# Routed sums in a PSUM bank of their own, and the blocks of additions, the value copy and the output addition at other places

## What is computed

```
# attention: 16 heads, window of 64 tokens, 16 numbers per head and token ("bond")
disp  = xn @ W_disp ; val = xn @ W_val
strain[t, d] = disp[t - 63 + d] - disp[t]                     # d = 0..63
bond    = gelu(strain @ W_strain + rel_pos_emb[d] @ W_pos) @ W_bond
damage  = sigmoid(gelu(strain @ W_dmg + b_dmg) @ W_dmg_out + b_dmg_out)
weights = softmax over d of (bond - 10 * damage)              # masked where t - 63 + d < 0
out     = (sum over d of weights * val[t - 63 + d]) @ W_cproj

# experts: 160, the 8 best of each token
gate  = top-8 of sigmoid(xn @ router_w.T + expert_bias), normed, * 2.5
h     = silu(xn @ w_gate[e])
routed[t] = sum over its 8 experts of gate * (h @ w_down[e])  # plus one shared expert
```

## Time and profile before

| | |
|---|---|
| median of 3 runs | 3710.76 us (3703.95 to 3714.79) |
| the profiled execution's own time | 3708.35 us |
| its span, first to last instruction | 3706.8 us |
| mean granted TensorE clock | 0.844 of full speed |
| busy share of the span: TensorE, VectorE, ScalarE, GpSimd | 67%, 77%, 67%, 63% |

### The profile page before, as it was taken

One profiled execution on the slowest core, in us unless ns is written; L12 is line 12 of the kernel. 1 busy time (PEld: TensorE's weight loads), 2 busy tenths in 40 slices (PEclk: granted clock), 3 DMA queues, 4 the chain that ended last, 5 costly groups with the idle time before them and its releaser, 6 DMA issues. The chain is left out here.

```text
span 3706.8 us, 64220 instructions
## 1 busy us (share of the span) xinstructions
PE 2501.0 (67%) x21226; PEld 1211.9 (33%) x21226; DVE 2861.7 (77%) x4254; ACT 2500.9 (67%) x1716; POOL 2327.2 (63%) x1604
## 2 busy tenths in 40 slices
PE   4662666776676766767888885566666676667666
PEld 2441112222222222246666661122222222222224
DVE  6888988888888888822433337999999899989981
ACT  1111979988888888843333337878878877778883
POOL 1222888678787878823343437777777777667771
PEclk9886879888888898868999997878778877878885
DMA  6773122222222222226878872222222222222222
GB/s 247 284 277 129 38 78 84 90 88 85 68 86 86 84 97 76 77 89 195 243 243 244 242 241 74 70 78 73 81 70 84 71 82 76 75 82 78 77 69 88
DMA packets 366243, 435.33 MB, mean 117 GB/s; under 512 B 48673, under 2 KB 282993, under 8 KB 366066
## 3 DMA queue, kind: packets, MB, share of 16 engines
q1 hardware_dynamic: 284658, 278.53, 24.0%
q0 software_dynamic: 57216, 143.22, 11.6%
q10 hardware_dynamic: 24192, 11.02, 1.1%
HBM read 233.83 MB, written 198.77 MB: 117 GB/s over the span
## 5 line engine op out<-in xcount | busy, mean ns | idle before, releaser
L1069 DVE SCALAR_TENSOR_TENSOR u_dve<-s_win,rpos,ps_here 128x512 f32<-128x512 f32 x1792 | 1197.6, 740 | 213.4 <-PE ps_l L1153 107.6
L1153 PE MATMUL ps_l<-u_dve,wsel 128*32 128x512 f32 x6144 | 984.8, 770 | 392.6 <-ACT u_dve L993 186.1
L927 POOL TENSOR_TENSOR u_pool<-s_win 128x4096 f32<-128x4096 f32 x128 | 1021.7, 7982 | 7.5 <-DMA s_win<-s_dram 5.3
L993 ACT ACTIVATE u_dve<-u_dve 128x4096 f32<-128x4096 f32 x224 | 809.9, 3616 | 56.8 <-DVE u_dve L1069 56.7
L1064 DVE TENSOR_TENSOR u_dve<-s_win,ps_here 128x4096 f32<-128x4096 f32 x160 | 703.3, 4412 | 43.1 <-PE ps_l L1153 43.1
L915 POOL DMA_INDIRECT yg<-yslot_dram,slot_now x512 | 485.6, 948 | 285.7 <-issue 148.5
L906 POOL DMA_INDIRECT xslot_dram<-xr,slot_now x512 | 494.6, 966 | 147.0 <-issue 143.6
L991 ACT ACTIVATE u_pool<-u_pool,bdmg_sb 128x4096 f32<-128x4096 f32 x128 | 474.5, 3707 | 66.1 <-POOL u_pool L927 66.1
L991 ACT ACTIVATE u_dve<-u_dve,bdmg_sb 128x4096 f32<-128x4096 f32 x128 | 474.4, 3706 | 15.8 <-DVE u_dve L1064 15.5
L1153 PEld LDWEIGHTS ps_l<-u_dve,wsel 128*32 128x32 f32 x6144 | 194.8, 128 | 842.8 <-issue 549.8
L1014 ACT ACTIVATE at_sb<-ps_u 128x512 f32<-128x512 f32 x256 | 151.0, 590 | 375.3 <-PE ps_u L1216 301.7
(11 more groups left out here) (142 smaller groups left out, 3011.1 us busy)
## 6 DMA issues: line engine op xcount, KB each, us to landing
band<-band_dram SPq DMA_DIRECT2D x32, 2048.0 KB
xslot_dram<-zero SPq DMA_DIRECT2D x16, 2688.0 KB, 9.1
xs<-xslot_dram SPq DMA_DIRECT2D x168, 256.0 KB, 3.6
yslot_dram<-ys POOLq DMA_DIRECT2D x168, 256.0 KB, 3.2
band_dram<-ml SPq DMA_DIRECT2D x64, 512.0 KB
we<-in_w_expert SPq DMA_DIRECT2D x336, 64.0 KB, 2.8
s_win<-s_dram SPq DMA_DIRECT2D x64, 288.0 KB, 5.9
s_dram<-s_sb POOLq DMA_DIRECT2D x16, 1024.0 KB, 4.7
```

Source lines behind the costliest of these rows:

```text
L927: pool.tensor_tensor(item_buffer(n), windows(par, ty, d0, 8), s_win[:, par, ty, PAD:PAD + TC].unsqueeze(1).to_broadcast([P, 8, TC]), ALU.s ...
L993: act.activation(u, u, ACT.Gelu).then_inc(gelu_done, 1)
L1069: last = dve.scalar_tensor_tensor(out=item_buffer(n)[:, d, :], in0=s_win[:, par, ty, d0 + d + 1:d0 + d + 1 + TC], scalar=rpos[:, d0 + d:d0 ...
L1153: last = pe.matmul(ps_l[32 * g:32 * g + 32, cgrp % 2, ty, :], wsel[:, ty, q, :], item_buffer(n)[:, d, :], start=(q == 0), stop=(q == 3))
```

## The change

Three things, all in `attend`. First, the damage logits get a single bank `ps_d` instead of two of `ps_l`, and the bank that is left over is `ps_acc`. TensorE's first damage product of a group waits for the tanh of the group before, and ScalarE does that tanh ahead of gelu n (n % 4 = 1) instead of behind it. Second, `add_routed` starts its sums with a multiplication into `ps_acc`, adds there, and ends each pair with one addition of `ps_acc` to `acc`, ahead of which (no longer at the start) it waits for the base; a pair counts 17 on `sum_round` instead of 16. Pair 1 moves from n = 11 to n = 7, and pair 0 from n = 3 to n = 15 of the step before. Third, on GpSimd the value copy moves from n = 3 to n = 7, and the output addition from n = 5 to n = 12.

```diff
-            ps_l = c.enter_context(nc.psum_tensor(f"ps_l_{half}", [P, 2, 2, TC], F32))
+            ps_l = c.enter_context(nc.psum_tensor(f"ps_l_{half}", [P, 2, TC], F32))
+            ps_d = c.enter_context(nc.psum_tensor(f"ps_d_{half}", [P, TC], F32))
+            ps_acc = c.enter_context(nc.psum_tensor(f"ps_acc_{half}", [P, J, C], F32))
...
+            ROUND = 2 * TOPK + 1
...
 # store_routed (SyncE); route on GpSimd, bring and gates on ScalarE count in the same way
-                        if some(NS * (t - 1)):
-                            sp.wait_ge(sum_round, NS * (t - 1))
+                        if some(2 * ROUND * (t - 1)):
+                            sp.wait_ge(sum_round, 2 * ROUND * (t - 1))
...
 # GpSimd
-                            if "a" in st and n == 3 and par == 0:
+                            if "a" in st and n == 7 and par == 0:
                                 spread(it - 1)
-                            if "y" in st and n == 5:
+                            if "y" in st and n == 12:
...
 # ScalarE: the same block, behind the gelu of item n before, ahead of it now
+                            if n % 4 == 1 and ("i" in st if n > 1 else "s" in st):
+                                k = 4 * s + cgrp - 1
+                                act.wait_ge(item_done, 4 * k + 4)
+                                if some(k - 1):
+                                    act.wait_ge(logits_in, k - 1)
+                                act.activation(tanh_sb[:, (cgrp - 1) % 2], ps_d[:], ACT.Tanh,
+                                               bias=hbout[:], scale=0.5).then_inc(tanh_done, 1)
...
 # VectorE, add_routed
                         if pair == 0:
-                            if some(16 * t):
-                                dve.wait_ge(base_in, 16 * t)
-                            if some(t):
-                                dve.wait_ge(gates_here, t)
+                            dve.wait_ge(gates_here, t)
                         for j in (2 * pair, 2 * pair + 1):
-                            if some(16 * TOPK * t):
-                                dve.wait_ge(gathered[j], 16 * TOPK * t)
+                            dve.wait_ge(gathered[j], 16 * TOPK * t)
+                        before = 2 * ROUND * (t - 1) + ROUND * pair
                         for m in range(2 * TOPK):
                             j = 2 * pair + m % 2
                             i = j * TOPK + m // 2
-                            if m >= 2:
-                                dve.wait_ge(sum_round, NS * (t - 1) + 2 * TOPK * pair + m - 1)
-                            dve.scalar_tensor_tensor(
-                                out=acc[:, old, j, :], in0=yg[:, i, :], scalar=gate_now[:, old, i:i + 1],
-                                in1=acc[:, old, j, :], op0=ALU.mult, op1=ALU.add).then_inc(sum_round, 1)
+                            if m < 2:
+                                dve.tensor_scalar(ps_acc[:, j, :], yg[:, i, :], gate_now[:, old, i:i + 1], None,
+                                                  ALU.mult).then_inc(sum_round, 1)
+                            else:
+                                dve.wait_ge(sum_round, before + m - 1)
+                                dve.scalar_tensor_tensor(
+                                    out=ps_acc[:, j, :], in0=yg[:, i, :], scalar=gate_now[:, old, i:i + 1],
+                                    in1=ps_acc[:, j, :], op0=ALU.mult, op1=ALU.add).then_inc(sum_round, 1)
+                        if pair == 0:
+                            dve.wait_ge(base_in, 16 * t)
+                        dve.wait_ge(sum_round, before + ROUND - 1)
+                        dve.tensor_tensor(acc[:, old, 2 * pair:2 * pair + 2, :], ps_acc[:, 2 * pair:2 * pair + 2, :],
+                                          acc[:, old, 2 * pair:2 * pair + 2, :], ALU.add).then_inc(sum_round, 1)
...
 # VectorE, step
-                            if half == 1 and "s" in st and n % 8 == 3:
-                                add_routed(s - first, 1 - par, n // 8)
+                            if half == 1 and "s" in st and n == 7:
+                                add_routed(s - first, 1 - par, 1)
+                            if half == 1 and "i" in st and n == 15:
+                                add_routed(s - first + 1, par, 0)
...
 # TensorE
-                                if n % 4 < 2:
+                                if n % 4 == 0:
                                     if some(4 * s + cgrp - 1):
                                         pe.wait_ge(logits_in, 4 * s + cgrp - 1)
+                                if n % 4 == 1:
+                                    if some(4 * s + cgrp):
+                                        pe.wait_ge(tanh_done, 4 * s + cgrp)
                                 pe.wait_ge(gelu_done, NI * s + n + 1)
...
-                                    last = pe.matmul(ps_l[32 * g:32 * g + 32, cgrp % 2, ty, :], wsel[:, ty, q, :],
+                                    logit = ps_d if ty else ps_l[:, cgrp % 2]
+                                    last = pe.matmul(logit[32 * g:32 * g + 32, :], wsel[:, ty, q, :],
                                                      item_buffer(n)[:, d, :], start=(q == 0), stop=(q == 3))
```

More of the change, by code:

```diff
@@ L911, in route @@
                             if some(s - first):
-                                pool.wait_ge(sum_round, NS * (s - first - 1) + 2 * TOPK * (j // 2 + 1))
+                                pool.wait_ge(sum_round, 2 * ROUND * (s - first - 1) + ROUND * (j // 2 + 1))
                                 pool.sem_inc(held, 1)
@@ L956, in bring @@
                         else:
-                            if some(NS * (s - first - 1)):
-                                act.wait_ge(sum_round, NS * (s - first - 1))
+                            if some(2 * ROUND * (s - first - 1)):
+                                act.wait_ge(sum_round, 2 * ROUND * (s - first - 1))
                                 act.sem_inc(held, 1)
@@ L993, in step @@
                                     act.activation(u, u, ACT.Gelu).then_inc(gelu_done, 1)
[L995 to L1001, removed]
                             if n == 13 and "i" in st and (not isinstance(s, int) or s + 1 < end):
@@ L1083, in step @@
                                                          in0=tanh_sb[:, (cgrp - 2) % 2], scalar=-5.0,
-                                                         in1=ps_l[:, (cgrp - 2) % 2, 0], op0=ALU.mult,
+                                                         in1=ps_l[:, (cgrp - 2) % 2], op0=ALU.mult,
                                                          op1=ALU.add).then_inc(logits_in, 1)
```

## The result

| | before | after |
|---|---|---|
| median of the runs, us | 3710.9 | 3666.2 |
| ratio after / before, 95% interval | | 0.9883 [0.9854, 0.9913] |
| profiled execution, own time / span | 3708.35 / 3706.8 | 3657.13 / 3655.7 |
| first half, 13 steps | 1025.2 | 1037.7 |
| second half, first Exp to last but one, 14 steps | 1229.2 | 1169.2 |

The change saves 45 us in the medians, 51 in the profiled executions; the prediction was 46. But it does not come as forecast: the second half gains 60 us, and the first half, which was to stay as it is, loses 12.5. The rest of the program (from one half to the other, start and end) is 3.6 us shorter.

The account below looks back on a forecast made before the run. It took the second half as bound by VectorE's gapless stretch including pair 1 (10.02 us), then ScalarE's gelu chain. Terms 104 - 72 + 14 = 46 us saved gave 3665 us on the median's scale; range 3628 to 3704.

Parts of the forecast that it names:

- Pairs at 4.8 us: VectorE's additions in the second half: with sums in PSUM, no hold-up, 4.8 us a pair (4.8 to 7.2).
- rival (a): VectorE's additions: writing PSUM is slow, up to 36 us less gain, 3701; chance 0.14.
- Pair 1 leaves n = 11, +104: Spot after the third `ml`, second half: removing pair 1 saves its time less 2.8 a step, 104 us.
- Pair 1 at n = 7, -72: Between subtractions 6 and 8, VectorE's gapless stretch: pair 1 costs 15 x 4.8 = 72 us, to 108.
- Pair 0 at n = 15, +14: Leaving n = 3 wins 2.0 us in seven odd steps; the wait for `ps_here` covers the new place: 14 us.
- Tanh before gelu, 0: ScalarE: delay at n = 9 covered by the band-transpose wait; at most 0.6 a step elsewhere, 19 us; taken as 0.
- Rival (c): Tanh order lands on the path, 3.2 us in 32 steps, 102 us slower, 3767; chance 0.06.
- GpSimd's moves and the windows, 0: GpSimd loses three waits and runs ahead; windows land just in time, then some 9 us earlier: 0.
- Rival (b): Windows come late for TensorE, `ps_here` waits 4.5 us in odd steps, 63 us more, 3728; chance 0.10.
- Rival (e): GpSimd's lateness was on the path, up to 66 us more gain, half of it gives 3632; chance 0.12.
- Rival (d): Additions still held: pair 1 at n = 7 costs 9.7 + 0.5, 81 us more, 3746; chance 0.03.
- Of what was to show it: Second-half signs: 4.8 us pairs, none over 0.5, band wait about 5, no `ps_here` wait, steps 85; first half 78.9.

Follow-up runs that it names:

- 1: Changed kernel with both pairs back at n = 3 and 11, sums still in PSUM: ratio 0.9867 to before, median 3658.5 us.
- 2: Kernel before with only the pairs moved to the new places, sums in SBUF: ratio 1.0121 to before, median 3756.2 us.
- 8: As 5, but pair 1 back at n = 11, pair 0 staying at n = 15: ratio 0.9748 to before, median 3615.1 us.
- 10: As 8, but tanh ahead of the gelu in the first half: ratio 0.9823 to before, median 3640.4 us.
- 5: Changed kernel with the first half as before (two damage banks, tanh behind gelu, GpSimd's steps back): ratio 0.9831 to before, median 3646.2 us.
- 6: Changed kernel with two damage banks in the first half again: ratio 0.9879 to before, median 3665.0 us.
- 7: As 5, but both pairs back at n = 3 and 11, sums in PSUM: ratio 0.9786 to before, median 3632.4 us.
- 3: Changed kernel with GpSimd's value copy back at n = 3 and output addition at n = 5: ratio 0.9874 to before, median 3663.9 us.
- 9: As 8, but GpSimd's value copy and output addition moved to n = 7 and 12 in the first half: ratio 0.9755, median 3615.0 us.
- 12: As 8, but pair 1 at n = 12, right behind the last `ml`: ratio 0.9748 to before, median 3610.4 us.

## Why the prediction was right, and where it was not

The total was right: 46 forecast, 45 measured in the medians. That it came so close was luck: two misses, 14 us more gain in the second half and 12.5 lost in the first, offset each other. The mechanism of the gain was right, and one step failed, tanh before the gelu.

- **Pairs at 4.8 us:** 4.58 at n = 7, 4.67 at n = 15 (2719.70 to 2724.37), never held. Spacing (3.70 - 0.349) / 13 = 0.258, as in SBUF; rival (a) falls. The cause of the hold-up is now shown by 1 and 2, where the prediction had only inferred it. (An element takes 1.03 ns by the prediction's own numbers, not 1.02; nothing hangs on it.) The Trainium skill (SBUF — State Buffer, "Who interferes with whom") says the same, and these runs agree: 13.32 us against 4.58 at the same place. By the Trainium skill (VectorE: DVE Perf Modes, "The TRN2 errata"), with its 62 cycles more for a PSUM source, a pair would have been an estimated 1 us longer; the spacing shows none of it.
- **Pair 1 leaves n = 11, +104:** third `ml` to copy falls from 12.36 to 5.13, 7.2 a step; forecast 6.9.
- **Pair 1 at n = 7, -72:** from one Exp to the third `ml` it takes 60.55 in kernel 8 and 64.89 in after, 4.3 a step (4.0 by the means of 8 to 10 and of after, 5 and 6); forecast 4.8.
- **Pair 0 at n = 15, +14:** kernel 7 to 8, 14 us by the ratios, 17 by the medians, 11 by the means of the profiles (1152.5 for 1 and 7, 1141.2 for 8 to 10). Right.
- **Second half in sum:** 60 measured, 46 forecast. No step of it failed; those above came out a few tenths of a us better per step, and from the copy to the Exp another 0.3 (13.8 to 13.5). GpSimd's lead is not the reason (3).
- **Tanh before gelu, 0: the step that failed.** The prediction looked at n = 9, where the wait for the band transposes covers it, and that holds: tanh's 6.63 us there and the copy's 5.58 stand in the place of one wait of 13.32. "At most 0.6 per step elsewhere" was the miss: tanh holds back gelus 13, 1 and 5 as well, with nothing to cover it, and the 1.2 us lost by gelu 6 are not won back at n = 9. Measured: 13 to 18 us in 13 steps, 25 us of the medians (10 against 9; 20 in 5 against after, which takes back all three edits). 1.0 to 1.4 a step is over the bound of 0.6 too. Rival (c) named the right edit, but by n = 9 and on the condition that the waits at the band copies vanish, which they do not (50.0 us in kernel 10's 13 steps); its price (3.2 a step, 102) was far too high.
- **GpSimd's moves and the windows, 0:** right (3, 9). Rival (b) is a real mechanism, and 12 shows it, but not here. Rival (e) falls.
- **Rival (d), 81 more:** the mechanism at the new places costs 110 (2 against after; 2 also leaves tanh, the bank and GpSimd as before).
- **Left on the table:** the prediction's own terms said that pair 1 costs 4.8 - 2.8 = 2.0 at n = 11 and 4.8 at n = 7, thus that its move loses 42 us once the hold-up is gone. Measured: 27 in the profiles (mean of 8 to 10 against after, 5 and 6), 31 in the medians of 5 and 8. I had the numbers and did not say so.

Of what was to show it: no long addition, 4.8 us pairs, the wait of 13 us down to 5.58, and no VectorE wait for `ps_here` all came. Second-half steps are 83.8 instead of 85, first-half steps 79.8 instead of 78.9.

## What to carry to other kernels

In this kernel an addition with two SBUF inputs on VectorE is held to the end of the GpSimd instruction beside it (up to 8.07 us before); accumulating in PSUM costs about the same per instruction (0.258 us of spacing against 0.262) and ends it, and then the place is to be chosen anew by what lies beside it, not by what was bad before. Wherever an instruction is moved ahead of another that feeds TensorE, price its own duration at every spot of the step, not only at the one with the longest wait. Before a slow product behind it is laid to the move, look for the same product in other executions: here it was as slow without the move. Sharing a buffer to free a bank can be kept to the phase that needs the bank: with the first half left as it was and pair 1 at its old place, the same idea gives 0.9748 instead of 0.9883.

## What the runs showed of the hardware that was not expected

- A held addition ends 0.15 to 0.16 us after GpSimd's instruction, in 16 of 16 cases before. Where two GpSimd instructions stand in a row, both things occur: in kernel 2 one addition ends between them (1.28 and 8.21 us) and the next is held again (1.41 and 8.25 us), in the kernel before one addition of 1.98 us, at 2405.15, is held over the end of a subtraction and the whole value copy behind it.
- Products 13 and 14 of one step took 3.48 and 1.92 us behind 3.48 us of idle time on TensorE (before), 3.64 and 3.64 behind 4.06 (kernel 10), but also 3.64 and 3.64 behind 3.23 (kernel 7): the idle time just before them does not tell the level by itself.
- The same first-half code took 1037.7 us in one execution and 1051.7 in another, with all other engines equally busy (VectorE 888.0 and 888.3) and TensorE 721.3 and 744.6, at 0.86 and 0.83.
